# Ranking tower on one core: ten more of the 26 embedding tables looked up by one-hot matmuls, and the pair products packed into four chunks

## What is computed

```python
e = stack([tbl_n[ids[:, n]] for n in range(26)], axis=1)      # 512 x 26 x 128, fp32
combined = concatenate([dense[:, None, :], e], axis=1)        # 512 x 27 x 128
inter = einsum('bfd,bgd->bfg', combined, combined)[:, iu, ju] # iu < ju: 351 pairs
h = concatenate([dense, inter, dense], axis=1)                # 512 x 607
h = maximum(h @ W_top1 + b_top1, 0)                           # 512
h = maximum(h @ W_top2 + b_top2, 0)                           # 256
y = h @ W_top3                                                # 1
```

## Time and profile before

| | |
|---|---|
| times of three executions | 151.48, 151.61, 152.4 us; median 151.61 |
| span of the profiled execution | 152.9 us, 1.3 us above that median |
| mean granted TensorE clock | 0.866 of full speed |
| busy, share of the span | PE 75%, PEld 62%, POOL 55%, DVE 33%, ACT 33% |
| end of the last one-hot lookup | about 54 us |
| first and last gather issued | 2.97 us, 111 us |

### The profile page before, as it was taken

The page is one execution under the profiler, slowest core; times in us unless marked ns, Lnnn a source line. Parts: engine busy times, 40 slices in busy tenths (PEclk is TensorE's granted clock), DMA queues, the critical chain, the costliest instruction groups (busy, mean ns, idle before and its releaser), DMA issues.

```text
span 152.9 us, 3980 instructions
## 1 busy us (share of the span) xinstructions
PE 115.3 (75%) x1789; PEld 95.1 (62%) x1789; DVE 51.1 (33%) x88; ACT 49.8 (33%) x98; POOL 83.9 (55%) x91
## 2 busy tenths in 40 slices
PE   0339401999379965599899899958999949995993
PEld 0127201677157654486788788647989739994691
DVE  6665600076457810712103800234500405104100
ACT  5045203368499840703000800204500106104011
POOL 4777777777787877777777777777710000000000
PEclk9999955569978999557999999997799996999659
DMA  1684447999644322221222221122210000000000
GB/s 43 151 192 164 166 164 227 270 248 238 172 166 167 119 53 57 50 57 51 55 53 56 58 51 51 51 56 56 60 30 0 0 9 0 4 4 0 4 0 1
DMA packets 5547, 12.82 MB, mean 84 GB/s; under 512 B 2025, under 2 KB 3049, under 8 KB 5277
## 3 DMA queue, kind: packets, MB, share of 16 engines
q0 software_dynamic: 2688, 5.51, 15.2%
q1 hardware_dynamic: 2832, 7.05, 15.0%
q10 hardware_dynamic: 10, 0.01, 0.0%
HBM read 12.56 MB, written 0.00 MB: 82 GB/s over the span
## 4 chain that ended last, share of the span: by engine, by line
PE 57%; DMA 25%; DVE 7%; issue 7%; ACT 2%; SPq 1%; ACTq 0%
DMA table_sb<-tbl 25%; PE h_ps L539 17%; PE gram_ps L511 9%; PE h_ps L563 7%; PE h_ps L534 6%; PE fill_ps L485 5%; DVE zT L391 5%; PE gram_ps L462 3%; PE gram_ps L539 3%; PE gram_ps L464 3%; DVE featT L385 2%; ACT featT L301 1%; PE gram_ps L534 1%; PE h_ps L573 1%; DVE h L396 1%
## 5 line engine op out<-in xcount | busy, mean ns | idle before, releaser
L289 POOL DMA_INDIRECT gathered<-tbl,ids_sb x84 | 83.1, 989 | 26.9 <-issue 25.3
L539 PE MATMUL h_ps<-zT,w_inter_sb 122*128 122x128 f32 (+1 forms) x196 | 29.2, 295 | 1.6 <-DVE zT L391 1.6
L539 PEld LDWEIGHTS h_ps<-zT,w_inter_sb 122*128 122x128 f32 (+1 forms) x196 | 27.3, 203 | 4.7 <-DVE zT L391 1.9
L462 PE MATMUL gram_ps<-onehot,table_hi 125*128 125x512 f32 x40 | 20.8, 519 | 4.8 <-DVE table_lo L424 4.7
L314 ACT ACTIVATE zT<-gram_ps 26x224 f32<-26x224 f32 (+4 forms) x40 | 12.1, 302 | 37.7 <-PE gram_ps L511 36.9
L418 DVE TENSOR_TENSOR onehot<-h_ps,rowno 125x1536 fp32r<-125x1536 f32 x10 | 17.5, 1755 | 17.8 <-PE gram_ps L464 16.9
L511 PE MATMUL gram_ps<-featT 128*26 128x26 f32 (+2 forms) x1280 | 15.5, 188 | 9.0 <-issue 5.8
L391 DVE COPY zT<-gram_ps 26x224 f32<-26x224 f32 (+4 forms) x40 | 12.9, 323 | 24.6 <-PE gram_ps L511 23.5
L511 PEld LDWEIGHTS gram_ps<-featT 128*26 128x26 f32 (+1 forms) x1280 | 13.2, 102 | 11.9 <-issue 7.5
L464 PE MATMUL gram_ps<-onehot,table_lo 125*128 125x512 f32 x40 | 19.6, 490 | 0.0
L307 ACT ACTIVATE featT<-fill_ps 128x512 f32<-128x512 f32 (+1 forms) x14 | 9.1, 656 | 26.4 <-PE fill_ps L485 26.4
(11 more groups left out here) (33 smaller groups left out, 55.5 us busy)
## 6 DMA issues: line engine op xcount, KB each, us to landing
table_sb<-tbl SPq DMA_DIRECT2D x5, 500.0 KB
w_inter_sb<-w_inter SPq DMA_DIRECT2D x1, 1792.0 KB, 29.9
gathered<-tbl,ids_sb POOLq DMA_INDIRECT x84, 3.8
oh_ids_sb<-oh_ids SPq DMA_DIRECT2D x1, 1000.0 KB
w_dense_sb<-w_dense SPq DMA_DIRECT2D x1, 512.0 KB, 25.0
w_sb<-w SPq DMA_DIRECT2D x1, 512.0 KB, 26.8
dense_sb<-dense SPq DMA_DIRECT2D x1, 256.0 KB, 23.2
oh_ids_sb<-oh_ids SPq DMA_DIRECT2D x1, 250.0 KB
```

The lines of the kernel that those rows point to most:

```text
L289: pool.indirect_dma_start(out=gathered[:, t, pos - GATHERED[0], :], out_offset=None, in_=tables[table], in_offset=bass.IndirectOffsetOnAxi ...
L462: nc.tensor.matmul(lookup_ps(k), table_hi[:, k % 2, rows], onehot[:, c, :], start=(c == 0), stop=False)
L539: last = nc.tensor.matmul(layer1_ps(t, n), w_inter_sb[0:k, c, units], zT[0:k, c, tile], start=False, stop=(c == CHUNKS - 1), skip_group_ch ...
```

## The change

Fifteen tables are looked up by one-hot matmuls: the twelve of 1000 rows (padded on the host to 1024, 128 partitions x 8 chunks) and three of 1250 (padded to 1280, 10 chunks). Eleven stay gathered (44 gathers). The masks now have two buffers, the split tables three. `featT` has 32 places per row; 5 of its vectors stand there twice, so that the pair products fit in 4 full chunks of 128 instead of 7.

Extracts of the new kernel, with comments added and several calls to a line:

```diff
-ONEHOT_TABLES = (0, 1, 3, 6, 8)
+ONEHOT_TABLES = (0, 1, 3, 6, 7, 8, 11, 12, 13, 14, 21, 15, 16, 18, 20)
+LARGER = (7, 13, 21)          # 10 chunks, the others 8
+RAW_BUFS = 3
+ROW_BUFS = 3
+SPLIT_BUFS = 3
+IDS_BUFS = 3
+PAUSE = 320
 # SP, per table k: load, then ids over 128 partitions
+            sp.dma_start(table_sb[k % RAW_BUFS][:, 0:table_cols(k)], rows)       # waits for the split of k-3
+            sp.dma_start(ids_all[:, k % IDS_BUFS, 1, :], oh_ids[k].partition_broadcast(P))  # for the masks of k-3
 # POOL, behind each gather
+                        if pauses > 0:
+                            pool.wait_ge(paused, pauses)
+                        pool.memset(scratch[:, :], 0.0).then_inc(paused, 1)      # 128 x 320
 # DVE, table k: low part, then masks of two chunks each
+            def compare_two(k, c):     # ids_all[.., 0, :] holds ids + 1, [.., 1, :] the ids
+                nc.vector.tensor_scalar(onehot[k % 2][:, c:c + 2, :], ids_all[:, k % IDS_BUFS, :, :],
+                                        row_number(rowno, k, c + 1), None, ALU.is_equal)
+            for k in range(ONEHOTS):
+                if k > 0:
+                    low_parts(k)                       # waits for the high part
+                    dve.wait_ge(next_ids_ready, k)
+                if k >= 2:
+                    dve.wait_ge(lookup_done, k - 1)
+                for c in range(0, dve_chunks(k), 2):   # k = 0: single chunks, low part in two halves
+                    compare_two(k, c)
 # ACT, table k
+                if dve_chunks(k) < row_chunks(k):
+                    compare_last(k)                    # k even: two chunks, 2 Abs of 512, 1 Relu of 1024
+                next_ids(k + 1)                        # ids + 1, Relu with bias 1
+                high_parts(k + 1)
+                elif k % 2 == 1:
+                    pair_to_featT((k - 3) // 2)        # two lookups in one copy of 1024; twice for two pairs
 # PE after the lookups (part of the order)
+            fill(1, 0); products(0, 0); products(0, 1); layer1_dense(1); fill(1, 1); fill(1, 2); products(0, 2)
+            fill(2, 0); products(0, 3); fill(2, 1); fill(2, 2); products(1, 0); layer1_dense(0); products(1, 1)
+            fill(3, 0); fill(3, 1); products(1, 2); layer1(0, 0); products(1, 3); layer1(0, 1); products(2, 0)
+            layer1(0, 2); layer1(0, 3); products(2, 1); fill(3, 2); products(2, 2); layer1(1, 0); layer1(1, 1)
+            ...
+            layer1(2, 3); layer1(LAST, 0); layer1(LAST, 1); layer2(2); layer1(LAST, 2); layer1(LAST, 3)
+            layer2_last(0); layer2_last(1); layer3(0, LAST); layer3(LAST, 1)
```

More of the change, by code:

```diff
@@ L50 @@
[L50 to L82, removed]
@@ L85, in groups_of_stage @@
[L85 to L96, removed]
+LAST = TILES - 1
+ONEHOT_TABLES = (0, 1, 3, 6, 7, 8, 11, 12, 13, 14, 21, 15, 16, 18, 20)
+LARGER = (7, 13, 21)
+ONEHOTS = len(ONEHOT_TABLES)
+SHORT, LONG = 8, 10
+FIRST = SHORT // 2 * DIM
@@ L97, in tower @@
+def tower(nc, dense, ids, oh_ids, tables, w_inter, w_dense, small, w2, out):
     fp32, fp32r, i32 = mybir.dt.float32, mybir.dt.float32r, mybir.dt.int32
@@ new lines, in _ @@
+            fill(1, 0)
+            products(0, 0)
+            products(0, 1)
+            layer1_dense(1)
+            fill(1, 1)
+            fill(1, 2)
+            products(0, 2)
+            fill(2, 0)
+            products(0, 3)
+            fill(2, 1)
+            fill(2, 2)
+            products(1, 0)
+            layer1_dense(0)
+            products(1, 1)
+            fill(3, 0)
+            fill(3, 1)
+            products(1, 2)
+            layer1(0, 0)
+            products(1, 3)
@@ new lines, in _ @@
+            layer1(0, 1)
+            products(2, 0)
+            layer1(0, 2)
+            layer1(0, 3)
+            products(2, 1)
+            fill(3, 2)
+            products(2, 2)
+            layer1(1, 0)
+            layer1(1, 1)
+            products(2, 3)
+            layer2(0)
+            products(LAST, 0)
+            layer1(1, 2)
+            products(LAST, 1)
+            layer1(1, 3)
+            layer1_dense(LAST)
+            products(LAST, 2)
+            layer1_dense(2)
+            products(LAST, 3)
@@ new lines, in _ @@
+            layer1(2, 0)
+            layer1(2, 1)
+            layer1(2, 2)
+            layer2(1)
+            layer1(2, 3)
+            layer1(LAST, 0)
+            layer1(LAST, 1)
+            layer2(2)
+            layer1(LAST, 2)
+            layer1(LAST, 3)
+            layer2_last(0)
+            layer2_last(1)
+            layer3(0, LAST)
+            layer3(LAST, 1)
+def first_layer_layout(w1):
+    w = np.zeros((P, ZCHUNKS, HID1), w1.dtype)
+    placed = set()
+    for q in range(4):
+        for c in range(ZCHUNKS):
+            for r in range(QUAD):
+                column = ABOVE[q][c] if r < CUT[q] else BELOW[q][c]
+                other = r if r < FEATS else COPIED[r - FEATS]
+                lo, hi = sorted((FIELD_AT[column], FIELD_AT[other]))
+                if lo != hi and (lo, hi) not in placed:
+                    placed.add((lo, hi))
+                    pair = lo * FEATS - lo * (lo + 1) // 2 + (hi - lo - 1)
+                    w[QUAD * q + r, c] = w1[DIM + pair]
+    assert len(placed) == FEATS * (FEATS - 1) // 2
```

716 lines of the change are left out of this document (411 added, 305 removed).

## The result

The changed kernel takes 126.34 us (median of 4 runs, 126.06 to 127.3) against 151.9 us for the kernel before (4 runs, 151.48 to 152.4): a ratio of 0.833, 95% interval 0.828 to 0.838, so 17% less. The forecast was 133 us with a range of 120 to 147. The profiled execution took 126.06 us, with a span of 124.3. In this and all later runs, those of the kernel before included, the time is 1.8 to 2.6 us above the span.

What follows compares the result with a forecast made beforehand. Kernel before bound first by arrival of tables and ids, from 54.2 us by PE. Lookups 73.1 + later PE work 46.1 + waits 13 + end 2.2 = 134.4 us span, so 133 us; forecast 126 to 141, 8-in-10 range 120 to 147.

Steps and rivals of the forecast that it cites:

- Lookups end at 73.1 us: Lookup matmuls: lookup 0 done at 12.5, plus 56.4 of PE work and 4.2 for hand-overs (0.3 a table).
- The mask of 1024: 0.69 us: VectorE's one-source mask in the lookups: 0.69 us priced by reads, 1.22 if priced by elements written.
- The cast row: Profile row for a VectorE cast, 625 elements in 0.73 us, read as speaking for the mask's upper price.
- rival 3: Masks in the lookups cost 1.22 us by elements written, VectorE paces, total 153 us; chance 0.08.
- The double copy of lookups: ScalarE's copy of a lookup to two places: taken at 1.1 us, between 1.05 and 2.40.
- The pauses cost VectorE nothing: GpSimd memsets behind gathers: no cost taken for VectorE because it has 3 us of cover, up to 11 us possible.
- Gathers 2.1 us apart: GpSimd gathers: 2.1 us each during lookups, 1.7 after; PE waits 5 us for them.
- Rival 2: POOL starves: gathers 2.8 us apart, PE stands 19 instead of 5 us, total 147 us; chance 0.18 (141 to 152).
- PE's work after the lookups: 46.1 us: Products 12.3, layer 1 16.1, dense matmuls 4.0, layer 2 7.4, transposes 4.2, layer 3 2.1 at full clock.
- Waits of 13 us after the lookups: Behind the lookups: 1 for copies before the first product, 4 half clock, 3 tail hand-overs, 5 gathers.
- The rival "without friction": Three engines overlap fully and gathers are in time: 121 us, range 117 to 125; chance 0.13.
- Rival 4: Tables arrive no faster than before, 6 us a table and ids; lookups end at about 93, total 150; chance 0.06.

Runs made afterwards that it cites:

- Kernel 1: Changed kernel with the GpSimd memset behind each gather left out: 123.58 us, 0.802 of the kernel before.
- kernel 3: Changed kernel with GpSimd's gathers started only after the first fourteen lookups, tile 0's transposes behind lookup 13: 171.4 us (one run).
- kernel 2: Changed kernel with two memsets behind each gather instead of one: 138.3 us, 0.905 of the kernel before.
- Kernel 7: Changed kernel with all four parts of a tile's products in a row on TensorE, not interleaved with layers: 133.37 us, ratio 0.882.
- Kernel 5: Changed kernel with tables and spread ids on 125 partitions again instead of 128: 170.36 us, 1.127 of the kernel before.
- Kernel 6: Kernel before with its five tables padded to 1024 rows on 128 partitions and ids spread over 128: 141.76 us against 152.17.
- Kernel 8: Changed kernel with seven chunks of z per layer 1 block instead of four (chunks 0 to 2 twice): 135.89 us, ratio 0.896.
- kernel 12: Kernel before with a contiguous copy of the dense features that layer 1 reads: 223.47 us against 226.66 on the same chip, ratio 0.986.
- kernel 10: Changed kernel without memsets, run again on a chip where the kernel before took about 225 us: 147.36 us.

## Why the prediction was right, and where its terms were off

**Lookups end at 73.1 us: 73.2 measured.** The sum held, two of its terms less so. The first matmul started at 5.7 us, not 7, and lookup 0 ended near 12.2, not 12.5. PE's 56.4 us of matmuls and transposes were right to the pitch (0.23). From 12.2 to 73.2 us they leave 4.6 us, where I had added 4.2 for hand-overs; for 2.7 of them PE is seen waiting for masks.

**The mask of 1024: 0.69 us, bounds to 1.22.** An undisturbed one lasts 0.74 us and its successor starts 0.66 to 0.68 us later. The price drawn from the two-input subtraction (same reads, same rate) came out, though no run shows that it is the reads which set it. The cast row misled, and rival 3, the slower case, fell. The double copy of lookups was taken at 1.1 and took 1.14.

**The pauses cost VectorE nothing: this step failed.** The memsets added 7.4 us to the masks (kernels 1 and 3), within my bound of 11, and some 3 us of it lay on the path. That it did not show in the lookups' end is luck of sizes: the 0.3 us a table for hand-overs was a guess, and the wait for held masks found room in it. The 3 us of cover that I gave as the reason were not there: VectorE was busy for 58.3 of 60 us. The Trainium skill, SBUF — State Buffer, section "Who interferes with whom", has the rule that VectorE in a two-port mode and GpSimd lock each other out for a whole instruction, and that whoever comes first holds. The sizes agree (+0.43 us for a memset of 0.38, and +0.42 us for a memset in kernel 2). The order agrees only in part: a memset that is lengthened in kernel 2 does have the mask before it, but each long mask has its recorded start before that of the memset as well. And 44 gathers left the masks at 751 ns against 748 without any.

**Gathers 2.1 us apart, PE waits 5 us for them: too careful.** They started 1.75 to 1.8 us apart in the lookups for the most part (for instance 17.92, 19.67 and 21.47) and 1.5 to 1.9 after; the last one started at 79.5 us, and PE waited for none. Rival 2 fell, but with a thin margin: kernel 2 lengthens the step by one memset and gets 138.3 us, over half of the way to the 147 of that rival.

**PE's work after the lookups: 46.1 us.** From 73.2 to 122.4 us are 49.2 us. Without the 2.7 us of issue gaps and the 0.4 us copy before the first product 46.1 are left. The single terms sit close as well: a part of products 0.7 to 0.9 us, four dense matmuls 0.89 to 1.09, layer 2 1.79 to 1.98.

**Waits of 13 us after the lookups: this is the term that was mis-sized; 3 measured.** I had scaled it from the 22 us that the kernel before lost between its work and its path. Four parts of it were guesses, and all were too large. Half clock was put at 4 us, and the clock stayed at 1.00 there. The wait for gathers was put at 5, and there was none. The tail's hand-overs were put at 3, and the order hides them: layer 1 and 2 follow each other from 107.07 us to the end without a gap. The first product was put at 1, and took 0.8. What remains are the gaps in the products for which the profile shows no cause, 2.7 us. Kernel 7 shows why they are small: with the same work in long rows they are 9.0. The rival "without friction" (121 us) was right in this part, and wrong in the other: the lookups did not end 4 us sooner. The measured 126.3 is a little nearer to it than to 133, at the lower edge of the 126 to 141 that the forecast claimed.

**The tables arrive faster: right, and what all else needs.** Rival 4 fell at 249 GB/s. Kernel 5 gives the price from the other side: 44 us for three partitions. The prediction called the DMA engines of the kernel before half idle; at a share of 0.72 they were a good quarter idle, and half idle is what kernel 5 shows (0.44). Kernel 6 shows that by itself it is worth 10.4 us to the kernel before, since gathers then bind. That the changed kernel can use more of it because it has 40 gathers fewer is an argument from these waits; no run changes the number of gathered tables alone.

**From span to time.** I took 1.3 us off the span of 134.4, reading the profiled span of the kernel before against the median time. But the time is 1.8 us above the span, in the runs of the kernel before too, so the sum should have read 136. It also means that the profiled execution of the kernel before, with its span of 152.9, took some 154.7 us, about 3 more than the median. The true span was 124.3, 10.1 us under mine, which is the 10 us of the waits above.

**Where the 25.6 us came from.** Between the two profiled spans lie 28.6 us; 3 of them are the long execution in which the kernel before was profiled. The lookups end 19 us later (73.2 against 54.2), and what stands behind them is 47.6 us shorter (51.1 against 98.7). PE's records, counted from start to start, say how these divide: the chunks of z 33.5 to 15.7 us, the dense matmuls 8.9 to 4.2, transposes 10.7 to 4.5, products 14.8 to 12.4, layer 2 with the same 64 records 12.7 to 7.5, and standing idle 14.1 to 3.0. What the clock gave (0.88 before, 1.00 after) is in all of these; in layer 2, where the work is the same, nothing else is known to have changed. Kernel 8 puts about 10 of the first 18 us down to the number of chunks, and kernel 12 has 3.2 to 4.2 for the contiguous dense copy.

**A better version.** Kernel 1 is the fastest found: 123.58 us, 0.802 of the kernel before.

## What to carry to other kernels

Price an unknown instruction from the nearest row with the same reads, state the other bound, and check what a second engine does to it: an instruction that only fills time on GpSimd can cost VectorE more than it lasts. Don't scale the lost time of an old kernel onto a new one; name each wait, and ask whether the new order of work already hides it. When tables arrive late at half idle DMA engines, look at the number of partitions before anything else, and see which transfer binds next.

## What the runs showed of the hardware

- Loaded over 125 partitions, a table and its ids took 7.3 us, and the kernel 44 us more than with 128 (kernel 5), with DMA engines busy for 0.44 of the time.
- A memset on GpSimd of 0.38 us lengthened a mask on VectorE by 0.43 us when it started 0.23 to 0.30 us behind it, and a mask lengthened a memset by 0.42 us (kernel 2); an indirect gather of 1.2 us beside a mask left it at 0.74 us. The gather itself grew: mean 954 ns in kernel 3, where VectorE is idle for most of the time, 1034 beside masks and low parts, 1181 with memsets between.
- In rows of 80 and more small matmuls (32 x 27) there are gaps of 1.4 to 2.2 us in which PE waits for nothing the profile shows; larger matmuls between them bring these from 9.0 to 2.7 us (kernel 7).
- On two chips the kernel before took 225 and 227 us instead of 152, the changed one without memsets 147 instead of 124, with waits named "remote" and a mean clock of 0.73 (kernel 12) and 0.95 (kernel 10). The cause was not settled.
